# A graph attention and convolution kernel on one core: 136 more columns of el gathered by GpSimd, 34 fewer batches of picks on TensorE

## The chip, the cores and the metric

The kernel runs on one core of a Trainium2 chip. The metric is the device time of one execution in microseconds (us); lower is better. The engines are TensorE (PE, with its weight loads as PEld), VectorE (DVE), ScalarE (ACT), GpSimd (POOL) and SyncE (SP). A "q" behind an engine's name (SPq, POOLq) stands for its sequencer, which issues DMAs.

## The reference

A graph of 6250 nodes with 512 features and 100000 edges, sorted by dst, goes through one attention layer and two convolution layers. What matters for this change is the attention score of every edge:

```python
el = jnp.einsum('nhf,hf->nh', feat_src, attn_l)      # 6250 x 8, one row per node
er = jnp.einsum('nhf,hf->nh', feat_dst, attn_r)
e = el[src] + er[dst]                                # 100000 x 8, one row per edge
e = jnp.where(e >= 0, e, NEG_SLOPE * e)
e_max = jax.ops.segment_max(e, dst, num_segments=N)
exp_e = jnp.exp(e - e_max[dst])
denom = jax.ops.segment_sum(exp_e, dst, num_segments=N)
a = exp_e / jnp.maximum(denom[dst], 1e-16)
msg = feat_v[src] * a[:, :, None]
rst = jax.ops.segment_sum(msg, dst, num_segments=N)
```

After it come layer norm, relu and two layers of `segment_sum((x @ W)[src] * norm, dst)`. The change touches only how `el[src]` is fetched.

## The kernel before, in words

The 100000 edges (padded to 100096) lie as 128 partitions by J = 782 columns; partition p holds edges 782p to 782p + 781. The 6250 nodes are 49 tiles of 128. `el[src]` is an array of 128 x 782 x 8 in the tile `edge`, and it is filled column by column, in two ways:

- **Picks** (columns 0 to PCOLS - 1, PCOLS = J - GCOLS = 764). Four columns (Q) make a batch, so there are 191 batches. SP loads the batch's source numbers, low nine bits, to all partitions (`rows_wmat<-low_tab`, L1107, four buffers). DVE makes three of the four one-hot tiles from them (L683), ACT the fourth (L1371, L1375). PE multiplies them with the table of el, split in three bf16 parts: 4 columns x 4 one-hots x 3 parts = 48 matmuls of 128x128 by 128x104 (L1618), into one of four PSUM banks (the profile's `mm`, `mm`, `tr`, `tr`). DVE then masks the result with the high bits of the source number (L689, semaphore `el_masked`) and reduces it to 8 numbers per edge (L696). DVE and ACT make one-hots up to two batches ahead of PE.
- **Gathers** (columns PCOLS to J - 1, GCOLS = 18). GpSimd issues one indirect DMA per column that fetches 128 rows of 8 numbers from the DRAM table `el_tab` (`collect`, L1236).

The picks stand between a head and a tail. In the head, x is normalised, el and er of each node are made, and the first 14 of 49 "values" (`feat_v` of one tile, L1563) are computed. After the picks, PE goes on with the values, and DVE has the long chain: er spread by scans (L766), scores (L775, L776), a segmented running maximum forwards (L784, then `top_local` for the late columns) and backwards (L798), exp, sums (L809, L822) and the weights. `scores` and the forward scan go over the picked columns first (`early`) and the gathered ones then (`late`), behind `all_landed(dve, el_in, GCOLS)`. Only then do the three large gather-and-add stages start (L1277), one indirect DMA of GpSimd per 128 edges.

What sets the order is the order of each engine's own instructions, written out by hand, with semaphores between engines. Each engine's loop over the batches is a real loop over four batches at a time, with the first batches and the last ones (what does not fill four) written out before and behind it (`pipelined`, L115). GpSimd's queue around the picks is: 18 gathers of el, 49 scatters of er (L1245), four gathers of dst (L1225), one of carry (L1250), `collect(EARLY, GCOLS)`, which is empty, as EARLY = GCOLS, then a wait for the first carry of the DVE chain and a memset (L1255). SP's queue is: 191 loads of low_tab, with the load of er (L1105) ahead of load 104; then three small tables written to DRAM (L1111, L1113) and read back (L1084 to L1089), for which it waits until all gathers of el have landed. The small tables are written in pieces of four bytes.

Of the kernel before, what the change touches and what calls it, by code (L numbers as in the profile page):

```python
# [68 lines left out]
GROUPED = (0, 8, 24, TILES)  # L69
XACT = 3  # L70
AHEAD = 8
GCOLS = 18
PCOLS = J - GCOLS
PB = -(-PCOLS // P)
Q = 4
ZW = 184
KT = 4
NA = -(-TILES // KT)
EARLY = GCOLS
V1 = 14  # L80
V_AT = (V1 + 11, V1 + 19, V1 + 29)
EXP_AT = (V1 + 25, V1 + 25)
# [39 lines left out]
def build(nc, x, src, dst, W_src, b_src, W_dst, b_dst, W_val, b_val, attn_l, attn_r, W1, b1, W2, b2, out):  # L122
    ctx = ExitStack()
    with ctx:
# [192 lines left out]
        def first(t):  # L317
# [39 lines left out]
        low_kept, src_hot_set, el_summed, a_hot_set, el_masked, el_picked = map(sem, (  # L357
            "low_kept", "src_hot_set", "el_summed", "a_hot_set", "el_masked", "el_picked"))
# [38 lines left out]
        def all_landed(eng, pair, count):  # L397
            for b in range(2):
                n = sum(1 for k in range(count) if k // AHEAD % 2 == b)
                if n:  # L400
                    eng.wait_ge(pair[b], 16 * n)
# [26 lines left out]
        def _(dve):  # L428
# [345 lines left out]
            def scores(at):  # L774
                did(dve.tensor_tensor(el[:, at, :], el[:, at, :], top[:, at, :], ALU.add))  # L775
                did(dve.scalar_tensor_tensor(el[:, at, :], el[:, at, :], SLOPE, el[:, at, :], ALU.mult, ALU.max))  # L776
# [9 lines left out]

            all_landed(dve, el_in, GCOLS)
            scores(late)
# [220 lines left out]
        def _(sp):  # L1009
# [71 lines left out]
            def load_tabs():  # L1081
                sp.wait_ge(ends_kept, 16)
                sp.wait_ge(tabs_kept, 48)
                sp.dma_start(ends_row[:, 0:UNITS], ends_tab).then_inc(tabs_in, 16)  # L1084
                for n in range(2):
                    sp.dma_start(slot_row[n], slot_tab[n].rearrange("b p -> (b p)")[0:SP].rearrange(
                        "(a n) -> a n", a=1)).then_inc(tabs_in, 16)
                with nc.allow_non_contiguous_dma(reason="the count of every second step"):
                    sp.dma_start(need_row, need_tab.rearrange("b p -> (b p)")[0:SP].rearrange(  # L1089
                        "(a n two) -> a n two", a=1, two=2)[:, :, 1]).then_inc(tabs_in, 16)  # L1090
# [19 lines left out]
            with nc.allow_non_contiguous_dma(reason="one step of the tables per partition"):  # L1110
                sp.dma_start(need_tab.rearrange("b p -> p b"), need_i[:, :]).then_inc(tabs_kept, 16)  # L1111
                for n in range(2):
                    sp.dma_start(slot_tab[n].rearrange("b p -> p b"), slotcol_i[n][:, :]).then_inc(tabs_kept, 16)  # L1113
            all_landed(sp, el_in, GCOLS)
            load_tabs()
# [64 lines left out]
        def _(pool):  # L1180
# [49 lines left out]

            def collect(lo, hi):
                for n in range(lo, hi):
                    if n % AHEAD == 0 and n >= 2 * AHEAD:
                        pool.wait_ge(el_in[n // AHEAD % 2], n // (2 * AHEAD) * (16 * AHEAD))
                    at = PCOLS + n
                    pool.indirect_dma_start(el[:, at, :], None, el_tab, bass.IndirectOffsetOnAxis(  # L1236
                        ap=src_flat[:, at:at + 1], axis=0)).then_inc(el_in[n // AHEAD % 2], 16)
            collect(0, EARLY)

            pool.wait_ge(er_idx_set, 1)  # L1240
            pool.wait_ge(er_zeroed, 16)
            for t in range(TILES):
# [7 lines left out]
            pool.indirect_dma_start(carry[:, :], None, er_node, bass.IndirectOffsetOnAxis(  # L1250
                ap=dst_i[:, 0:1], axis=0)).then_inc(er_first_in, 16)
            collect(EARLY, GCOLS)

            pool.wait_ge(dve_prep, marks["carry_in"][0])
# [484 lines left out]
```

## Time and profile before

| | us |
|---|---|
| median of 3 runs | 4226.9 |
| lowest and highest | 4221.7, 4226.94 |
| the profiled execution, its own time | 4226.32 |
| its span | 4224.4 |
| PE busy | 3556.3 (84%) |
| POOL busy | 2477.7 (59%) |
| DVE busy | 2342.3 (55%) |
| ACT busy | 1840.1 (44%) |

The span runs from the first to the last instruction of the trace. The page also cuts it into 40 slices of 105.6 us; a digit is the busy share of a slice in tenths. Timelines give the start of a row, its length, the engine, the line of the code, the operation with what it writes and reads, how many there are, and in brackets how long the engine idled before it and what ended that. The chain of waits goes back from the last instruction to whatever released each step.

### The profile page before, as it was taken

How to read it: one execution, taken by the hardware profiler on the slowest of the kernel's cores; microseconds unless marked ns; L12 is line 12 of the kernel's file. 1: busy time of each engine (PE TensorE's matmuls, PEld its weight loads, DVE VectorE, ACT ScalarE, POOL GpSimd, SP SyncE). 2: the span in 40 equal slices, each digit the busy share in tenths (PEclk: the TensorE clock that was granted, in tenths of full speed). 3: DMA queues.
4: the chain of work that ended last, by engine and by line, in shares of the span. 5: the costliest groups of instructions: out<-in, count | busy, mean ns of one | idle time of the engine just before them, and what ended most of it. 6: DMA issues, size and time to landing. Idle time of an engine off the chain costs nothing.

```text
span 4224.4 us, 59337 instructions
## 1 busy us (share of the span) xinstructions
PE 3556.3 (84%) x16793; PEld 1765.3 (42%) x16793; DVE 2342.3 (55%) x4085; ACT 1840.1 (44%) x4240; POOL 2477.7 (59%) x2597
## 2 busy tenths in 40 slices
PE   5899998677788888889678888888997778888887
PEld 4599994322223333344233333333443333333333
DVE  6598889577777888888222323333452222333336
ACT  4366551344545555545333334444343333444442
POOL 3620000277777777754677777777204777777775
PEclk9999999899999999999899999999999999999998
DMA  8722323577777777755777777777315777777779
GB/s 293 232 65 59 87 52 112 204 210 210 210 210 211 210 211 211 210 186 189 210 210 210 210 210 210 210 210 211 104 67 187 211 210 210 210 210 211 210 209 346
DMA packets 319071, 808.16 MB, mean 191 GB/s; under 512 B 69250, under 2 KB 98836, under 8 KB 317826
## 3 DMA queue, kind: packets, MB, share of 16 engines
q0 software_dynamic: 195328, 630.16, 51.3%
q1 hardware_dynamic: 93973, 121.41, 8.9%
q10 hardware_dynamic: 29580, 54.49, 3.7%
q8 instruction: 67, 1.10, 0.1%
q14 instruction: 123, 1.00, 0.1%
HBM read 718.41 MB, written 88.24 MB: 191 GB/s over the span
## 4 chain that ended last, share of the span: by engine, by line
PE 36%; POOL 23%; issue 20%; DMA 11%; DVE 6%; SPq 1%; POOLq 1%; DVEq 1%; ACT 1%; ACTq 0%
POOL edge L1277 18%; PE mm L1526 8%; PE mm L1618 5%; PE tr L1618 5%; DMA edge<-h_tab,src_group 5%; POOL rows_wmat L1277 5%; DMA rows_wmat<-v_tab,src_group 4%; PE sm L1690 4%; PE mm L1690 4%; PE sm L1563 3%; PE tr L1690 2%; DVE edge L865 2%; PE tr L1521 1%; PE hist_ps L1690 1%; DVE big L875 1%
## 5 line engine op out<-in xcount | busy, mean ns | idle before, releaser
L1277 POOL DMA_INDIRECT edge<-h_tab,src_group x1564 | 1483.8, 949 | 711.0 <-issue 447.8
L1433 ACT ACTIVATE hots<-iota,drel 128x128 f32<-128x128 f32 x1760 | 538.0, 388 | 1175.9 <-PE tr L1690 599.2
L1277 POOL DMA_INDIRECT rows_wmat<-v_tab,src_group x782 | 739.2, 945 | 288.2 <-issue 218.7
L1690 PE MATMUL mm<-edge,hots 128*128 x880 | 455.2, 666 | 196.4 <-SPq L1097 193.5
L1690 PE MATMUL sm<-edge,hots 128*128 x880 | 445.9, 654 | 159.8 <-SPq L1097 157.6
L890 DVE TENSOR_TENSOR big<-big,mm 128x512 f32 x220 | 151.2, 687 | 680.2 <-PE tr L1690 663.5
L890 DVE TENSOR_TENSOR big<-big,sm 128x512 f32 x220 | 151.2, 687 | 617.1 <-PE misc L1690 602.7
L1690 PE MATMUL tr<-edge,hots 128*128 x880 | 395.6, 592 | 0.0
L1690 PEld LDWEIGHTS mm<-edge,hots 128*128 128x128 f32 x880 | 179.6, 211 | 464.9 <-issue 464.8
L1526 PE MATMUL mm<-rows_wmat 128*128 128x512 f32 x784 | 355.7, 597 | 0.0
L1690 PEld LDWEIGHTS sm<-edge,hots 128*128 128x128 f32 x880 | 176.7, 208 | 421.5 <-issue 421.4
L1670 PE MATMUL mm<-edge,hots 128*128 128x512 f32 x592 | 275.9, 605 | 62.5 <-ACT hots L1419 39.8
L1670 PE MATMUL sm<-edge,hots 128*128 128x512 f32 x584 | 276.7, 604 | 54.8 <-issue 26.9
L865 DVE TENSOR_TENSOR edge<-rows_wmat,tr 128x1024 f32<-128x1024 f32 x224 | 271.9, 1214 | 85.4 <-SPq L1097 85.3
L1419 ACT ACTIVATE hots<-eler_hots,ones 128x256 f32<-128x256 f32 x440 | 223.6, 508 | 204.9 <-PE sm L1670 77.2
L865 DVE TENSOR_TENSOR edge<-rows_wmat,misc 128x1024 f32<-128x1024 f32 x216 | 262.5, 1215 | 81.4 <-SPq L1097 81.3
L1414 ACT ACTIVATE eler_hots<-iota,drel 128x128 f32<-128x128 f32 x880 | 298.2, 386 | 0.0
L1255 POOL MEMSET big<- 128x8781 f32 x1 | 7.4, 7423 | 449.5 <-DVE carry L723 449.5
L1690 PEld LDWEIGHTS tr<-edge,hots 128*128 128x128 f32 x880 | 167.3, 190 | 212.2 <-issue 212.2
L1436 ACT ACTIVATE hots<-hots,ones 128x1024 f32<-128x1024 f32 x220 | 252.6, 1148 | 7.1
L1618 PE MATMUL mm<-big,edge 128*128 128x104 bf16 x4608 | 226.8, 211 | 11.5 <-issue 6.0
L1618 PEld LDWEIGHTS mm<-big,edge 128*128 128x128 bf16 x4608 | 220.5, 98 | 13.3 <-issue 10.5
(255 smaller groups left out, 4814.8 us busy)
## 6 DMA issues: line engine op xcount, KB each, us to landing
h_tab<-rows_wmat SPq DMA_DIRECT2D x98, 256.0 KB, 2.0
edge<-h_tab,src_group POOLq DMA_INDIRECT x1564, 3.7
rows_wmat<-low_tab SPq DMA_DIRECT2D x191, 128.0 KB, 3.0
ht_tab<-rows_wmat SPq DMA_DIRECT2D x49, 256.0 KB, 4.4
big<-ht_tab ACTq DMA_DIRECT2D x49, 256.0 KB, 2.9
v_tab<-rows_wmat ACTq DMA_DIRECT2D x49, 256.0 KB, 2.9
x_tab<-big SPq DMA_DIRECT2D x49, 256.0 KB, 2.2
rows_wmat<-v_tab,src_group POOLq DMA_INDIRECT x782, 3.7
```

The costliest lines, as they stand in the source:

```text
L865: dve.tensor_tensor(msgs[:, k % MSGS, :, :].rearrange("p c (h f) -> p c h f", f=F), got, weights.unsqueeze(3).to_broadcast([P, 2, H, F]), ...
L890: dve.tensor_tensor(big[:, ds(o, D)], big[:, ds(o, D)], agg_ps[bank][:, :], ALU.add).then_inc(a["acc_added"], 1)
L1277: pool.indirect_dma_start(ring[:, 2 * u + c, :], None, tab, bass.IndirectOffsetOnAxis(ap=src_group[:, n:n + 1], axis=0)).then_inc(a["rows_ ...
L1414: act.activation(dist[:, n % 2, c, :], iota[:, :], ACT.Abs, bias=drel[:, n * 2 + c:n * 2 + c + 1], scale=-1.0).then_inc(a["dist_set"], 1)
L1419: act.activation(onehot[:, n % HOTS, :, :], dist[:, n % 2, :, :], ACT.Relu, bias=ones[:, 0:1], scale=-1.0).then_inc(a["onehot_set"], 1)
L1433: act.activation(group_hots[:, q % 2, e, :], iota[:, :], ACT.Abs, bias=drel[:, col:col + 1], scale=-1.0).then_inc(a["dist_set"], 1)
L1436: act.activation(group_hots[:, q % 2, :, :], group_hots[:, q % 2, :, :], ACT.Relu, bias=ones[:, 0:1], scale=-1.0).then_inc(a["onehot_set"], 1)
L1526: last = nc.tensor.matmul(bank, rows[:, slot, k * P:(k + 1) * P], rhs(k), start=(k == 0), stop=(k == KC - 1))
L1563: last = pe.matmul(sm[par][:, :], ht_ring[:, s.j, k * P:(k + 1) * P], wmat[:, k, 0:D], start=(k == 0), stop=(k == KC - 1))
L1618: last = pe.matmul(sum_ps[bank][:, q * NA * H:(q + 1) * NA * H], src_hot[:, par, kt, q * P:(q + 1) * P], el_parts[:, part, kt, :, :], star ...
L1670: last = pe.matmul(gat_ps[w % GAT_SUMS][:, :], onehot[:, w % HOTS, n, :], msgs[:, w % MSGS, n, :], start=(n == 0), stop=(n == 1))
L1690: last = pe.matmul(agg_ps[bank][:, :], group_hots[:, q % 2, w % GROUP * 2 + n, :], edge[:, ds(slot[w % OFFS] + n * D, D)], start=(n == 0), ...
```

## The change

GCOLS goes from 18 to 154, so PCOLS goes from 764 to 628 and the batches from 191 to 157. EARLY stays at 18 gathers ahead of the scatters. The other 136 gathers come behind the gather of carry, and each of them first waits until VectorE has masked a given number of batches: gather n (from 0) waits for n - 18 + 12 masked batches, so gather 18 for 12 and gather 153 for 147.

```diff
-GCOLS = 18
+GCOLS = 154
 PCOLS = J - GCOLS
 PB = -(-PCOLS // P)
...
-EARLY = GCOLS
+EARLY = 18
+PACED = 12
...
             def collect(lo, hi):
                 for n in range(lo, hi):
+                    if n >= EARLY:
+                        pool.wait_ge(el_masked, n - EARLY + PACED)
                     if n % AHEAD == 0 and n >= 2 * AHEAD:
                         pool.wait_ge(el_in[n // AHEAD % 2], n // (2 * AHEAD) * (16 * AHEAD))
                     at = PCOLS + n
```

GpSimd's instructions behind the scatters of er, before (the first row is the last of the 49 scatters; `dst_rows` and `er_node` are gathers of dst and of carry; the memset of `big` waits for the DVE chain behind the picks):

```order
L1245 DMA er_tab<-eler_hots,er_idx 106368x8 [waits er_scattered0]
L1225 DMA big<-dst_rows,gidx 128x256 [waits dve_prep]
L1225 DMA big<-dst_rows,gidx 128x256 x3
L1250 DMA carry<-er_node,edge 128x8 [waits dst_in,er_kept]
L1255 MEMSET big 128x8781 [waits dve_prep]
L1259 DMA edge<-w_tab,gidx 128x2048 [waits w_kept]
```

And after, the first rows and the last of them:

```order
L1253 DMA carry<-er_node,edge 128x8 [waits dst_in,er_kept]
L1239 DMA edge<-el_tab,src_flat 128x8 [waits el_masked] x6
L1239 DMA edge<-el_tab,src_flat 128x8 [waits el_in1,el_masked]
L1239 DMA edge<-el_tab,src_flat 128x8 [waits el_masked] x7
L1239 DMA edge<-el_tab,src_flat 128x8 [waits el_in0,el_masked]
L1239 DMA edge<-el_tab,src_flat 128x8 [waits el_masked] x7
...
L1258 MEMSET big 128x8781 [waits dve_prep]
L1262 DMA edge<-w_tab,gidx 128x2048 [waits w_kept]
```

All 136 gathers stand between the gather of carry and the memset; every eighth also waits for the landing of an earlier group of eight.

TensorE's end of the picks, before: the loop's last batch and branch, then the batches written out behind the loop, the turning of tables and the values.

```order
L1618 MATMUL tr<-big,edge 128x104 x48
L115 REGISTER_ALU
L115 COMPARE_AND_BRANCH
L1618 MATMUL mm<-big,edge 128x104 x96
L1618 MATMUL tr<-big,edge 128x104 x48
L1629 MATMUL tr<-ident,big 128x128 x8
L1563 MATMUL sm<-rows_wmat,big 128x512 x20
```

And after:

```order
L1621 MATMUL tr<-big,edge 128x104 x48
L116 REGISTER_ALU
L116 COMPARE_AND_BRANCH
L1621 MATMUL mm<-big,edge 128x104 x48
L1632 MATMUL tr<-ident,big 128x128 x8
L1566 MATMUL sm<-rows_wmat,big 128x512 x20
```

Behind the loop stands one batch where there were three; the loop itself turns 38 times where it turned 46 times.

SP's end of the loads, before (load 104 on, with er ahead of it, then the small tables):

```order
L1105 DMA big<-er_tab 128x6256 [waits er_scattered0,er_scattered1,far_dist,src_hot_set]
L1107 DMA rows_wmat<-low_tab 128x512
L1107 DMA rows_wmat<-low_tab 128x512 [waits far_dist,src_hot_set] x86
L1111 DMA need_tab<-need_i 128x4x1
L1113 DMA slot_tab_gat<-slotcol_i_gat 128x4x1
L1113 DMA slot_tab_gcn<-slotcol_i_gcn 128x4x1
L1084 DMA ends_row<-ends_tab 1x391 [waits ends_kept,tabs_kept,el_in1,el_in0]
```

And after:

```order
L1106 DMA big<-er_tab 128x6256 [waits er_scattered0,er_scattered1,far_dist,src_hot_set]
L1108 DMA rows_wmat<-low_tab 128x512
L1108 DMA rows_wmat<-low_tab 128x512 [waits far_dist,src_hot_set] x52
L1112 DMA need_tab<-need_i 128x4x1
L1114 DMA slot_tab_gat<-slotcol_i_gat 128x4x1
L1114 DMA slot_tab_gcn<-slotcol_i_gcn 128x4x1
L1085 DMA ends_row<-ends_tab 1x391 [waits ends_kept,tabs_kept,el_in1,el_in0]
```

The load of er stands at the same batch, 104; behind it 52 loads follow where 86 did.

## Rows read from the trace of the kernel before

**Rows 1.** The page: busy tenths in 40 slices of the span.

```profile
PE   5899998677788888889678888888997778888887
DVE  6598889577777888888222323333452222333336
POOL 3620000277777777754677777777204777777775
```

**Rows 2.** Timeline of PE: picks, two batches to a row, first, 51st pair.

```profile
202.25 6.06 PE L1618 MATMUL mm<-big,edge 128*128 128x104 bf16 x96 [2.90 <-ACT edge L1375]
208.15 4.59 PE L1618 MATMUL tr<-big,edge 128*128 128x104 bf16 x96
...
429.48 4.59 PE L1618 MATMUL tr<-big,edge 128*128 128x104 bf16 x96
```

**Rows 3.** Timeline of POOL: last scatter, last gather before the memset.

```profile
234.86 0.96 POOL L1245 DMA_INDIRECT er_tab<-eler_hots,er_idx x1 [0.30 <-issue]
...
241.19 0.94 POOL L1250 DMA_INDIRECT carry<-er_node,edge x1 [0.30 <-issue]
691.62 7.42 POOL L1255 MEMSET big<- 128x8781 f32 x1 [449.49 <-DVE carry L723]
```

**Rows 4.** Windows: length, then PE, PEld, DVE, ACT, POOL busy, PEclk, DMA share, GB/s.

```profile
210.00:236.00 26.00, 26.00 (x569) 26.00 (x566) 24.37 (x72) 15.73 (x24) 19.73 (x21) 1.00 0.26 64
250.00:276.00 26.00, 26.00 (x568) 26.00 (x566) 23.30 (x72) 15.89 (x24) 0.00 (x0) 1.00 0.27 60
```

**Rows 5.** Timeline of DVE: one-hots beside scatters, then a whole batch without.

```profile
219.41 1.13 DVE L683 TENSOR_SCALAR edge<-rows_wmat,low_id 128x512 bf16<-128x512 f16 x3
...
242.42 0.58 DVE L689 TENSOR_TENSOR rows_wmat<-mm,rows_wmat 128x416 f32<-128x416 f32 x1
...
611.09 0.88 DVE L683 TENSOR_SCALAR edge<-rows_wmat,low_id 128x512 bf16<-128x512 f16 x3 [0.23 <-PE mm L1618]
611.89 0.58 DVE L689 TENSOR_TENSOR rows_wmat<-mm,rows_wmat 128x416 f32<-128x416 f32 x1
612.39 0.57 DVE L696 TENSOR_REDUCE edge<-rows_wmat 128x416 f32 x1
612.88 0.20 DVE L675 TENSOR_TENSOR rows_wmat<-edge,iota 128x52 f32<-128x52 f32 x1
613.30 0.88 DVE L683 TENSOR_SCALAR edge<-rows_wmat,low_id 128x512 bf16<-128x512 f16 x3 [0.22 <-PE tr L1618]
```

**Rows 6.** The load of er at batch 104: SP issues, DVE and PE wait.

```profile
423.95 0.35 SPq L1105 DMA_DIRECT2D big<-er_tab  x1
434.94 0.88 DVE L683 TENSOR_SCALAR edge<-rows_wmat,low_id 128x512 bf16<-128x512 f16 x3 [3.28 <-DMA rows_wmat<-low_tab]
436.65 6.20 PE L1618 MATMUL mm<-big,edge 128*128 128x104 bf16 x96 [2.58 <-ACT edge L1375]
```

**Rows 7.** Timelines of SP and PE at the end of the picks.

```profile
620.04 0.51 SPq L1113 DMA_DIRECT2D slot_tab_gcn<-slotcol_i_gcn  x1
635.41 0.24 SPq L1084 DMA_DIRECT2D ends_row<-ends_tab  x1
...
624.17 0.93 PE L1618 MATMUL mm<-big,edge 128*128 128x104 bf16 x15
...
633.60 4.68 PE L1618 MATMUL mm<-big,edge 128*128 128x104 bf16 x52 [3.19 <-issue]
638.08 2.78 PE L1618 MATMUL tr<-big,edge 128*128 128x104 bf16 x48
643.25 1.19 PE L1629 MATMUL tr<-ident,big 128*128 128x128 f32 x8 [2.39 <-DVE big L739]
```

**Rows 8.** Timeline of DVE behind the picks: scores and scans, early and late.

```profile
659.43 6.52 DVE L775 TENSOR_TENSOR edge<-edge 128x6112 f32<-128x6112 f32 x1
...
673.62 13.23 DVE L784 TENSOR_TENSOR_SCAN edge<-big,edge 128x764 f32<-128x764 f32 x8
686.89 0.31 DVE L775 TENSOR_TENSOR edge<-edge 128x144 f32<-128x144 f32 x1
687.23 0.31 DVE L776 SCALAR_TENSOR_TENSOR edge<-edge 128x144 f32<-128x144 f32 x1
687.58 1.38 DVE L791 TENSOR_TENSOR_SCAN edge<-big,edge 128x18 f32<-128x18 f32 x8
```

**Rows 9.** Line L1236, the gathers of el: time to landing.

```profile
DMA to landing us min/median/max: 3.1/6.1/7.3
```

## The prediction

> **What bounds the kernel now.** The page's slices come first [rows 1]. PE is at 9 tenths or more from the third slice to the sixth, and these are the picks; GpSimd stands at zero there, while its slices behind the eighth are at 7, for it issues the large gathers there. So the stage that the change shortens is one in which PE is full and GpSimd is free, and no later stage lies beside it: the chain of waits passes through the picks on PE, batch after batch, then through VectorE's scans and scores, and only then into the gathers of L1277. Whatever the picks end earlier, everything behind them starts earlier, as long as nothing else is late. The second view is PE's timeline [rows 2]: between the pair of batches that starts at 208.15 and the one at 429.48 there are 50 pairs, 221.33 us, so 4.427 us a pair and 2.213 us a batch of 48 matmuls. In the windows PE is busy 26.00 of 26 us at a granted clock of 1.00, the upper of its two levels [rows 4]. VectorE is near its own limit: a batch of it goes from 611.09 to the end of L675 at 613.08, 1.99 us, with 0.22 us idle before the next [rows 5].
>
> **What the change removes.** 34 batches of picks. On PE they are 34 x 2.213 = 75.3 us, all on the path. VectorE's, ScalarE's and SP's share of these batches lies beside PE's and is worth nothing more.
>
> **What the picks' end adds to that.** The three batches behind the loop do not run at 2.213 us. PE starts the first of them at 624.17, hobbles through 48 matmuls with gaps that are put down to issue, has four of them left at 633.60, and ends the third at 640.86 [rows 7]: 16.7 us where 6.6 would do, a loss of 10.1. SP has just written the three small tables, in pieces of four bytes; its last write is issued at 620.04 and its wait for their landing ends at 635.41. I read the gaps as engines that leave their loops and want new code while DRAM is busy with these pieces. After the change SP's writes stand as far ahead of the last batch as before (it runs four buffers ahead), but only one batch stands behind the loop, so PE leaves the loop two batches, 4.4 us, later with respect to the writes. Two bounds: if the hobbling belongs to the exit, the single batch takes what the first one took, 634.0 - 624.2 = 9.8 us, a loss of 7.6 where it was 10.1, and the saving is 75.3 + 2.5 = 77.8. If it belongs to the writes, PE is released at the same distance from them, some 13.6 us behind 620.04, four matmuls before its end, so at about 634.0 in the old counting where the end was at 640.86: 75.3 + 6.9 = 82.2. The trace shows one case only, so neither is excluded; I take a value nearer to the first, 79, since PE's own gaps begin at the exit and not at the writes.
>
> **What the change adds on GpSimd.** 136 gathers. An indirect DMA of this kind holds GpSimd 0.94 us and the next follows 0.30 us later, 1.25 us each [rows 3], so one per batch of 2.213 us fits. GpSimd has nothing to do between 242.1 and 691.62, 449.49 us of idle time [rows 3], so this lies wholly in a hole. In order: carry is issued at 241.19; the mask at 242.42 is the 17th (the first is at about 207, one per 2.213 us), so gathers 18 to 22 or 23 go at once and the rest one per batch. The last one waits for 147 masks of 157: it is issued some ten batches, 22 us, before the picks end. These gathers have landed in 3.1 to 7.3 us [rows 9]. What waits for them: SP's reading back of the small tables, which is far from late, and VectorE's late scores, which come behind the early scans, 46 us behind the picks' end [rows 7, 8]. What is queued behind them on GpSimd is the memset at 691.62, which waits for VectorE anyway. Cost on the path: 0. If that cover were gone, each gather would cost 1.25 us at most.
>
> **What the gathers do to the picks beside them.** No gather of el runs beside picks in this trace, but 49 scatters of er and five gathers do at the start of the picks, at 1.27 us from one to the next, so 1.7 of them per batch. There PE is full all the same [rows 4]. VectorE is busy 24.37 us of 26 beside 21 of them and 23.30 without: 1.07 / 21 = 0.05 us each. With one per batch that is 0.05 us of the 0.22 us that VectorE has free, so 0 on the path. The other bound is the worst single case: three one-hots took 1.13 us where 0.88 is usual [rows 5], 0.25 us. The mask releases each gather, so all of them meet VectorE at the same point of its batch, and that could make the worst case the rule: 0.25 - 0.22 = 0.03 us by 136 is 4 us. I take 0 to 1 us, because the average of many positions is at 0.05. PE's and ACT's instructions are not longer in that window, and the DMA share is 0.26 beside 0.27, so the loads of low_tab are not slowed either.
>
> **The load of er** (3.1 MB) is issued at 423.95 at batch 104, before and after. The load of low_tab behind it comes late, VectorE waits 3.28 us and PE 2.58 us, and PE's next pair takes 6.20 us and not 4.43 at first [rows 6]: some 4.5 us. Five small gathers now fall beside it. They add little to 3.1 MB; between 0 and 2 us, I take 0.5.
>
> **Head and tail.** VectorE's conversions go over 628 columns and not 764, one transposition and one small DMA fall away in the head; PE works there on the values without waiting for them, so 0. Behind the picks the early part shrinks and the late part grows. Scores: 6112 numbers take 6.52 us and 144 take 0.31, 1.04 ns a number, so the sum stays. Scans: eight of 764 columns take 13.23 us and eight of 18 take 1.38 [rows 8], 1.99 ns a column, so the sum stays too. 0.
>
> **The sum**, against the profiled execution (4226.32 us, span 4224.4, 1.9 us around it; the median of the runs is 4226.9): 4226.3 - 79 + 1 = 4148.3. I forecast 4148.
>
> **A rule that speaks against the change.** The rows show VectorE's one-hots 0.05 us longer for each DMA of GpSimd beside them [rows 4, 5]. The Trainium skill, "SBUF — State Buffer", section "SBUF: two separate sides", says that VectorE and GpSimd share a pair of ports as an exclusive lock: who starts first keeps it for its whole instruction and the other "fully blocks", which in VectorE's two-port modes also starves the descriptors of GpSimd's DMAs. By that rule the sum could come out at the second rival's. The trace does not bear it out at full strength.
>
> **The rivals.**
> 1. *VectorE becomes the pace of the picks.* The gathers are phase-locked to the mask and each costs more than the 0.22 us that are free, say 0.25 to 0.40. Then 135 batches take 0.03 to 0.18 us more, 4 to 24 us: 4152 to 4172. For it: VectorE at 90% and the row of 1.13 us. Against it: 1.7 DMAs a batch did not slow PE. Chance 12%.
> 2. *Slower: GpSimd shuts VectorE out.* Each gather keeps VectorE's one-hots waiting for its whole 0.94 us. VectorE's batch is then 2.93 us, 0.72 us over PE's, by 136: 98 us against 78 saved, so 4246. It is slower than before from 0.58 us a batch over the free 0.22, that is from 0.80 us a gather on. For it: one engine at 90%, and a wait that puts the gather right before the one-hots. Against it: the windows, where the whole of 21 DMAs cost 1.07 us. Chance 3%.
> 3. *The change does not move the end.* The gathers come too late, because every eighth waits for a landing that the load of er holds back, and VectorE waits for the last of them. GpSimd would have to lose over 22 + 46 us for that. Or the picks end earlier and something else is late; I find nothing, as er has landed by 435 and the first picked tables are older. 2%.
> 4. *The end of the picks is cleaner still*: VectorE and ScalarE also leave their loops two batches later, and nobody stalls. Then 75.3 + 10.1 = 85: 4141. 10%.
>
> **How the numbers follow.** The forecast with its bounds (77.8 to 82.2 us saved, less 0 to 4 for contention and the load of er: 4144 to 4153) has 73%. To hold eight in ten I reach to 4140 for the fourth rival, and into the first as far as 4164. Below 4140 I see 4%, above 4164 some 9%. A difference of 0.2%, 8.5 us, is about what a measurement can tell from no change. Faster by more than that: the forecast, rivals 1 and 4, 95%. Within: half of the third and what of the first goes far beyond its bounds, 2%. Slower: 3%.
>
> **What would show it.** In the trace after: 157 batches at 2.21 us a batch in PE's timeline between 250 and 420, at a clock of 1.00; VectorE idle 0.15 to 0.2 us a batch; GpSimd's gathers 2.2 us apart, each released by VectorE's mask, the last at about 535; the picks' end at 559 to 563 and the memset of `big` at 612 to 614 where it was at 691.62; every stage behind it of unchanged length. Wrong would be: pairs of batches over 4.5 us with PE waiting for the one-hots of L683 (rival 1, or 2 if over 5 us); a wait at the load of er well over 3.3 us; a batch behind the loop that takes over 10 us.

## The result, and the profile after

The changed kernel takes 4150.4 us in the median of its four runs beside 4225.7 for the kernel before (a fourth run of it lowers the 4226.9 of the table above); the ratio is 0.9822, with a 95% interval of 0.9808 to 0.9836, so 75 us or 1.8% less. One of the four runs took 5913 us at a granted clock of 0.557; without it the median is 4148.8 (4143.5 to 4152.0), and such runs are left out of the numbers of e4 and e5 below. Forecast were 4148, a range of 4140 to 4164, and faster by over 0.2% with a chance of 95%. The profiled execution took 4152.04 us with a span of 4150.1. Run again on another chip (e0 below) the same kernel took 4148.5 us, at a ratio of 0.9821.

The page's slices answer to [rows 1]. PE's full stretch is shorter, and GpSimd, which stood at 2, 0 and 0 in the third to the fifth slice, is at 5, 4 and 4:

```profile
PE   5899988677888888898788888888997788888887
...
DVE  6599887677777888885222333333552222333336
...
POOL 3654411677777777654777777777106777777775
```

PE's timeline of the picks, in pieces, answers to [rows 2, 6, 7]: the first pair, two rows around the load of er, and the end. (A row is cut where the view's window ends: the pair at 442.37 is 45 matmuls long here.)

```profile
207.55 6.18 PE L1621 MATMUL mm<-big,edge 128*128 128x104 bf16 x96 [2.90 <-ACT edge L1378]
...
434.91 4.59 PE L1621 MATMUL tr<-big,edge 128*128 128x104 bf16 x96
442.37 2.87 PE L1621 MATMUL mm<-big,edge 128*128 128x104 bf16 x45 [2.87 <-ACT edge L1378]
...
550.21 4.59 PE L1621 MATMUL mm<-big,edge 128*128 128x104 bf16 x96
554.64 0.71 PE L1621 MATMUL tr<-big,edge 128*128 128x104 bf16 x12
555.64 0.78 PE L1621 MATMUL tr<-big,edge 128*128 128x104 bf16 x8 [0.29 <-issue]
556.84 0.22 PE L1621 MATMUL tr<-big,edge 128*128 128x104 bf16 x1 [0.42 <-issue]
557.82 2.46 PE L1621 MATMUL tr<-big,edge 128*128 128x104 bf16 x50 [0.76 <-issue]
564.26 2.32 PE L1621 MATMUL tr<-big,edge 128*128 128x104 bf16 x25 [3.97 <-issue]
566.38 4.11 PE L1621 MATMUL mm<-big,edge 128*128 128x104 bf16 x48
```

The picks run from 207.55 to 570.49, 362.9 us, where they ran from 202.25 to 640.86, 438.6 us. That is 75.7 us less, and 34 x 2.213 is 75.3: the batches are gone at their full price, and nearly nothing else happened. Over their ideal (157 x 2.213 = 347.5, before 191 x 2.213 = 422.7) the picks lose 15.4 us, before 15.9. The end of the picks was forecast to be cleaner; it is not. PE starts its last three batches at 554.64 and ends them at 570.49, 15.9 us where 6.6 would do; it was 16.7. From SP's last write of a small table to the end of the picks it is 20.0 us, and it was 20.8.

GpSimd's timeline answers to [rows 3]: carry, the first late gathers, the last ones and the memset.

```profile
246.31 0.94 POOL L1253 DMA_INDIRECT carry<-er_node,edge  x1 [0.30 <-issue]
247.55 0.94 POOL L1239 DMA_INDIRECT edge<-el_tab,src_flat  x1 [0.30 <-issue]
...
538.94 0.94 POOL L1239 DMA_INDIRECT edge<-el_tab,src_flat  x1 [1.40 <-DVE rows_wmat L690]
541.02 0.94 POOL L1239 DMA_INDIRECT edge<-el_tab,src_flat  x1 [1.14 <-DVE rows_wmat L690]
621.17 7.43 POOL L1258 MEMSET big<- 128x8781 f32 x1 [79.20 <-DVE carry L724]
```

Nearly every late gather waits 1.1 to 1.4 us for VectorE's mask, as the pacing wants, and the last one is issued 29 us ahead of the picks' end; 22 were worked out, and the halt at the end of the picks makes up the rest. The memset comes 70.5 us earlier than before. The 5 us that are missing there were lost ahead of the picks, which start at 207.55 and not at 202.25; in e0, which is the same kernel, they start at 201.56, and in the other kernels below between 201.95 and 205.48. So this is the scatter of executions and not the change.

VectorE's windows answer to [rows 4]; the columns are PE, PEld, DVE, ACT and POOL busy, granted clock, DMA share and GB/s:

```profile
302.00:416.00 114.00, 114.00 (x2476) 114.00 (x2474) 107.38 (x311) 68.89 (x104) 48.98 (x52) 1.00 0.28 61
```

PE is full at a granted clock of 1.00 throughout this window. VectorE is busy 94% of the time.

### The profile page after: what moved, and what is told of

Its sections match the earlier page's. It is cut to its first block, busy times and chain, and to the rows that moved or that the text cites. A ratio compares the mean times of both kernels' runs of the same rounds, so it can differ in the third digit from the quotient of the medians.

```text
span 4150.1 us, 55488 instructions
## 1 busy us (share of the span) xinstructions
PE 3489.9 (84%) x15160; PEld 1694.2 (41%) x15160; DVE 2288.9 (55%) x3880; ACT 1798.3 (43%) x4172; POOL 2607.4 (63%) x2733
## 3 DMA queue, kind: packets, MB, share of 16 engines
q14 instruction: 123, 1.01, 0.1%
## 4 chain that ended last, share of the span: by engine, by line
PE 34%; POOL 23%; issue 21%; DMA 12%; DVE 6%; SPq 1%; POOLq 1%; DVEq 1%; ACT 1%; ACTq 0%
POOL edge L1280 17%; PE mm L1529 8%; POOL rows_wmat L1280 5%; DMA edge<-h_tab,src_group 5%; DMA rows_wmat<-v_tab,src_group 4%; PE mm L1621 4%; PE sm L1693 4%; PE tr L1621 4%; PE mm L1693 4%; PE sm L1566 3%; PE tr L1693 2%; DVE edge L866 2%; PE tr L1524 1%; DMA ht_tab<-rows_wmat 1%; PE hist_ps L1693 1%
## 5 line engine op out<-in xcount | busy, mean ns | idle before, releaser
L1693 PE MATMUL mm<-edge,hots 128*128 x880 | 465.9, 679 | 195.3 <-SPq L1098 189.7
L1239 POOL DMA_INDIRECT edge<-el_tab,src_flat x154 | 147.5, 958 | 180.0 <-DVE rows_wmat L690 157.6
L1693 PE MATMUL hist_ps<-edge,hots 128*128 x440 | 206.8, 592 | 0.0
L1693 PE MATMUL misc<-edge,hots 128*128 x440 | 206.8, 592 | 0.0
```

The costliest lines, as they stand in the source:

```text
L1693: last = pe.matmul(agg_ps[bank][:, :], group_hots[:, q % 2, w % GROUP * 2 + n, :], edge[:, ds(slot[w % OFFS] + n * D, D)], start=(n == 0), ...
```

## The experiments

The question after the result was not whether the 34 batches are worth 75 us, but what of the other terms was luck: do the gathers really cost nothing, is the pacing of use, what makes the loss at the picks' end, and how far can it be taken? The theory: the gathers lie in GpSimd's hole and beside PE's picks for free. The rival: they cost a little and something else gives it back.

**e0: the change again**, on the chip of the next three.

> The changed kernel again, beside the others on the same chip: 4150 us, 75 under the kernel before. The gaps of PE, VectorE and ScalarE at the end of the picks begin about 5 us behind the last write of the small tables and cost 10 us, as in both traces so far.

Measured: 4148.5 us (4145.9 to 4150.3), ratio 0.9821 (0.9805 to 0.9838). The end of its picks, and SP's queue beside it:

```profile
548.54 0.50 PE L1621 MATMUL tr<-big,edge 128*128 128x104 bf16 x6
549.41 1.11 PE L1621 MATMUL tr<-big,edge 128*128 128x104 bf16 x20 [0.36 <-issue]
550.92 2.67 PE L1621 MATMUL tr<-big,edge 128*128 128x104 bf16 x49 [0.41 <-issue]
558.94 1.98 PE L1621 MATMUL tr<-big,edge 128*128 128x104 bf16 x21 [5.35 <-issue]
560.71 3.75 PE L1621 MATMUL mm<-big,edge 128*128 128x104 bf16 x48
```

```profile
544.41 0.51 SPq L1114 DMA_DIRECT2D slot_tab_gcn<-slotcol_i_gcn  x1
559.44 0.24 SPq L1085 DMA_DIRECT2D ends_row<-ends_tab  x1
```

PE halts in the two batches that are still in its loop (x6 to x21, 96 matmuls), 5 us behind the last write, and goes on at 558.94, half a microsecond before SP's wait ends. So the exit of the loop is not what it halts at: the exit comes behind the halt. The DMA engines are not busy while it lasts; the last columns here are the granted clock, the DMA share and GB/s:

```profile
547.50:558.50 11.00, 5.31 (x102) 4.77 (x99) 3.01 (x9) 1.76 (x3) 0.00 (x0) 0.92 0.00 0
```

So the packets of the writes are through by 547.3, and what SP waits for until 559.44 is not the moving of the 6 KB.

**e1: no late gathers.** 157 batches of picks, no gathers beside them.

```diff
-            collect(EARLY, GCOLS)
+            pool.memset(edge[:, (PCOLS + EARLY) * H:J * H], 0.0).then_inc(late_zeroed, 1)
```

> The 136 late gathers of el are left out and their columns are set to zero by one memset of GpSimd, so the scores of those edges are not the reference's; picks are 157 batches as in the change. My theory (the gathers lie in GpSimd's hole and cost the picks nothing): 4150, within 3 us of the change, with VectorE's busy time in 302 to 416 falling from 107.4 to about 102.6 us. The rival (the gathers slow the picks or the load of er): faster than the change by 5 us or more.

Measured: 4148.1 us (4146.5 to 4148.7), ratio 0.9818 (0.9802 to 0.9834), 0.4 us from e0. VectorE in the window:

```profile
302.00:416.00 114.00, 114.00 (x2477) 114.00 (x2474) 102.42 (x310) 68.33 (x104) 0.00 (x0) 1.00 0.23 59
```

So 136 gathers cost the path nothing that can be measured. They do cost VectorE something, 102.42 us busy without them and 107.38 with 52 of them, 0.095 each (0.12 in e0, 108.69), and this lies in its idle time.

**e2: no pacing.**

```diff
-                    if n >= EARLY:
-                        pool.wait_ge(el_masked, n - EARLY + PACED)
```

> The wait for el_masked is taken out, so the 136 gathers follow one another at 1.25 us, 1.8 to a batch, from about 247 to 417. My theory (the pacing is not needed, as VectorE has 0.22 us a batch free and a gather takes 0.05 to 0.09 of it): 4150, within 3 us of the change. The rival (VectorE becomes the pace once there are two gathers a batch): pairs of batches over 4.43 us between 250 and 417 and 4 to 20 us more than the change.

Measured: 4145.5 us (4144.6 to 4147.6), ratio 0.9813 (0.9797 to 0.983). GpSimd issues its last gather at 415.56 and not at 535 to 541:

```profile
302.00:416.00 114.00, 114.00 (x2477) 114.00 (x2474) 103.68 (x310) 68.98 (x104) 86.57 (x91) 1.00 0.33 63
```

There are 91 gathers in this window and not 52, and VectorE is busy less, 103.68 us: 0.014 us for each gather. That depends on how the gathers happen to fall on VectorE's batch: in the other kernels whose gathers run freely it is 0.025 (e5), 0.032 (e4), 0.037 (e6) and 0.053 (e9, 107.25 us in all, as much as in the change), and in the paced ones 0.094 (e3) to 0.12 (e0). The pacing is not needed. The difference of 3 us to e0 lies within the intervals, and the traces put it elsewhere: PE is full in this window in both, but in e2 the pair behind the load of er took 4.60 us at a granted clock of 1.00, where it took 6.20 at 0.72 in e0, and the halt at the end cost 7.5 us and not 9.3. So it isn't shown that the pacing costs time either.

**e6: two gathers to a mask.**

```diff
-                        pool.wait_ge(el_masked, n - EARLY + PACED)
+                        pool.wait_ge(el_masked, (n - EARLY) // 2 + PACED + 8)
```

> 154 gathers as in the change, but two of them released by every mask (from mask 20 to 87), so both lie at the same point of VectorE's batch. In the change each gather takes 0.09 to 0.12 us of VectorE's 0.22 free, unpaced ones 0.014. If it is the fixed phase that costs: VectorE's busy time rises to near 26 of 26 us between 260 and 390, pairs of batches stay at 4.43 us or go up to 4.5 (0 to 3 us on the time, 4148 to 4152). If it is the number of gathers that costs: as unpaced, 4146, with VectorE at about 23.6 of 26.

Measured: 4148.4 us (4145.2 to 4149.7), ratio 0.9817 (0.98 to 0.9833), VectorE 105.77 us in 302 to 416 beside 91 gathers, 0.037 each. The design was at fault: two gathers take 2.5 us and a batch 2.2, so GpSimd fell behind the masks and hardly waited for them. In effect it is a second unpaced kernel and says nothing on a fixed phase.

**e10: another phase.** One gather per batch, released by PE's end of the batch.

```diff
-                        pool.wait_ge(el_masked, n - EARLY + PACED)
+                        pool.wait_ge(el_summed, n - EARLY + PACED)
```

> The change with each late gather released by TensorE's end of the batch (el_summed) and not by VectorE's mask, so that it meets VectorE's one-hots from their start. If the phase sets what a gather takes from VectorE: its busy time in 302 to 416 leaves 107 to 108.7 us, up to 110 or more if the whole of the one-hots is met, down to 104 if the end of the gather was what met them; pairs of batches at 4.43 us as long as it stays under 114, and the time 4146 to 4152. If only the number of gathers matters: 107 to 108.7, as in the change.

Measured: 4148.3 us (4146.5 to 4149.8), ratio 0.9824 (0.9807 to 0.984), and in the window

```profile
302.00:416.00 114.00, 114.00 (x2477) 114.00 (x2474) 102.68 (x311) 69.16 (x104) 49.73 (x52) 1.00 0.29 61
```

VectorE is busy as without any gathers. It is the same number of gathers as in the change and they cost 0.005 us each and not 0.1, so it is the phase that sets what they take. The timelines show which part of a gather does it. First GpSimd and VectorE in e10, then in e0:

```profile
306.67 0.94 POOL L1239 DMA_INDIRECT edge<-el_tab,src_flat  x1 [1.60 <-PE mm L1621]
...
306.11 0.88 DVE L684 TENSOR_SCALAR edge<-rows_wmat,low_id 128x512 bf16<-128x512 f16 x3 [0.22 <-PE mm L1621]
```

```profile
307.33 0.94 POOL L1239 DMA_INDIRECT edge<-el_tab,src_flat  x1 [1.73 <-DVE rows_wmat L690]
...
307.38 1.01 DVE L684 TENSOR_SCALAR edge<-rows_wmat,low_id 128x512 bf16<-128x512 f16 x3
```

In e10 a gather starts while the one-hots run and outlives them; they take their 0.88 us. In e0 the one-hots start 0.05 us behind the gather, outlast it by 0.12, and take 1.01. The other batches of this window agree. In e10 the three one-hots nearly always start 0.16 to 0.27 us ahead of a gather and take 0.88 us in every batch. In e0 and in the change they nearly always start behind it: they take 1.02 to 1.10 us when they start 0.2 to 0.3 us behind, 0.88 at about 0.44, 1.08 to 1.12 from 0.47 to 0.5, and 0.95 to 0.98 from 0.6 on. That is what comes out if a one-hot (one every 0.3 us) that would start between some 0.45 and 0.7 us into a gather is held until 0.7. It is read from the rows; no run moved the gathers by known steps.

**e3: the small tables written later.**

```diff
+            sp.wait_ge(el_picked, PCOLS // Q)
             with nc.allow_non_contiguous_dma(reason="one step of the tables per partition"):
```

> SP writes the three small tables only after the last pick is reduced. If the loss of 10 us at the end of the picks belongs to these writes: the 157 batches run to their end at 2.21 us with no gap over 1 us, the picks end 9 to 10 us earlier, and the time is 4140 to 4145, less than the full 10 us since part of the halt then falls on VectorE's scans. If it belongs to the engines leaving their loops: the gaps stay where they are and the time is 4150.

Measured: 4140.3 us (4139.3 to 4143.4), ratio 0.98 (0.9783 to 0.9816), 8.2 us less than e0. The picks run to their end without a gap, and one stands later:

```profile
549.83 4.59 PE L1622 MATMUL tr<-big,edge 128*128 128x104 bf16 x96
554.26 2.38 PE L1622 MATMUL mm<-big,edge 128*128 128x104 bf16 x48
559.03 1.18 PE L1633 MATMUL tr<-ident,big 128*128 128x128 f32 x8 [2.39 <-DVE big L740]
560.04 13.90 PE L1567 MATMUL sm<-rows_wmat,big 128*128 128x512 f32 x32
582.03 5.41 PE L1567 MATMUL sm<-rows_wmat,big 128*128 128x512 f32 x8 [8.09 <-ACT rows_wmat L1362]
```

The loss goes with the writes and not with the loops. It falls now on ScalarE and, through it, on PE's values, 8.09 us, while VectorE is in its long scans and scores; of it 1.95 us reach VectorE (its wait for PE ahead of 587.99), and the rest is hidden.

**e7: every small table written twice.**

```diff
+                for copy in range(2):
+                    to = (need_tab, *slot_tab) if copy else spare_tab
+                    for tab, cols in zip(to, (need_i, *slotcol_i)):
+                        sp.dma_start(tab.rearrange("b p -> p b"), cols[:, :]).then_inc(tabs_kept, 16)
```

> The change with every one of the three small tables written twice, first to a spare place, at the same point of SP's queue. If the halt at the end of the picks is the time in which these writes land: the wait of SP grows from 15 us behind the last write to about 28, the picks end some 13 us later and the time is 4158 to 4164. If it belongs to the loops' exits: 4148 to 4150.

Measured: 4152.3 us (4149.5 to 4155.9), ratio 0.9831 (0.9815 to 0.9847), 4 us more than e6 on the same chip, where 10 to 16 (picks that end 13 us later) were forecast for the writes and none for the exits. SP goes on at 566.63, 24.4 us behind the start of its first write, where it was 16 in e0; but PE halts in 549 to 559, hobbles once more at 566 and ends at 567.3, some 3 us later than in e0. Its last three batches lose 13.3 us (547.34 to 567.31, where 6.6 would do), and kernels with one set lose 7.5 to 9.3. So the halt grows by 4 to 6 us where the wait grows by 8.4: it is not the time in which the writes land. The number missed; the direction stands in the traces, while the times just overlap e6's.

**e8: the same tables in larger pieces.** They are kept in DRAM by partition, 384 pieces of 16 bytes where there were 1536 of 4, at the same place of SP's queue; reading them back then takes 12 DMAs and not three.

```diff
-        need_tab = dram("need_tab", [CUT.blocks, P], I32)
+        need_tab = dram("need_tab", [P, CUT.blocks], I32)
...
-                sp.dma_start(need_tab.rearrange("b p -> p b"), need_i[:, :]).then_inc(tabs_kept, 16)
+                sp.dma_start(need_tab, need_i[:, :]).then_inc(tabs_kept, 16)
```

> The change with the three small tables kept in DRAM by partition, so that they are written in 384 pieces of 16 bytes and not in 1536 of 4 bytes, at the same place of SP's queue, and read back column by column. If the halt at the end of the picks comes from the number of small writes: SP's wait falls from 15 us behind the last write to about 5, the gaps shrink from 10 us to 3 or less, and the time is 4140 to 4143, as with the tables written later. If it comes from any write to DRAM at that point, or from the loops' exits: the gaps stay and the time is 4148 to 4150.

Measured: 4137.7 us (4136.3 to 4138.8), ratio 0.9799 (0.9782 to 0.9815), 10.6 us less than e10 on the same chip and 2.3 us under the range given. SP's queue, and PE beside it:

```profile
543.69 0.43 SPq L1116 DMA_DIRECT2D slot_tab_gcn<-slotcol_i_gcn  x1
547.95 0.24 SPq L1085 DMA_DIRECT2D ends_row<-ends_tab  x1
```

```profile
547.90 4.59 PE L1623 MATMUL tr<-big,edge 128*128 128x104 bf16 x96
552.33 2.37 PE L1623 MATMUL mm<-big,edge 128*128 128x104 bf16 x48
```

The wait falls from 15 us to 4.3 and the halt is gone. It is the small pieces and not a write at that place. The halt's share of the 10.6 us is 9.0 in the profiles (e10 loses 9.2 us in its last three batches, e8 0.2); another 1.6 is the pair behind the load of er, which ran at a granted clock of 1.00 here (4.60 us) and 0.72 in e10 (6.19 us). This pair took 4.60 us in e2, e6 and e7 too and 6.18 to 6.20 in every other kernel, so it goes with neither the gathers nor the writes. Here the tables are read back in pieces of four bytes, hundreds of them, from 548.23 on, and neither PE nor VectorE halts.

**e4: 238 columns gathered,** 136 batches of picks, unpaced (GCOLS = 238, and e2's edit).

> 238 columns gathered, 544 picked (136 batches), no pacing. My theory: 21 batches fewer than in the change at 2.213 us save 46.5 us more, with nothing lost to the gathers: 4148.5 - 46.5 - 1 (no phase lock) = 4101, range 4098 to 4106. The 220 late gathers at 1.25 to 1.26 us run from about 247 to 523, some 10 us past the end of the picks, which VectorE's er scans and early scores cover. The rival (GpSimd's end now sets the late scores, or VectorE becomes the pace): 4110 or more, with VectorE waiting for el ahead of the late scores.

Measured: 4107.5 us (4105.2 to 4108.3), ratio 0.972 (0.9701 to 0.974), on e6's chip, where 154 columns gave 4148.4: 40.8 us saved where 46.5 were forecast, and 1.5 us over the range given. The small tables are written at 497.92 here, while the late gathers still run, and the halt is longer:

```profile
499.79 1.78 PE L1619 MATMUL mm<-big,edge 128*128 128x104 bf16 x35
503.73 0.21 PE L1619 MATMUL mm<-big,edge 128*128 128x104 bf16 x1 [2.17 <-issue]
505.05 0.24 PE L1619 MATMUL mm<-big,edge 128*128 128x104 bf16 x1 [1.11 <-issue]
506.00 2.82 PE L1619 MATMUL mm<-big,edge 128*128 128x104 bf16 x28 [0.71 <-issue]
511.51 0.24 PE L1619 MATMUL mm<-big,edge 128*128 128x104 bf16 x1 [2.69 <-issue]
...
517.40 5.13 PE L1619 MATMUL tr<-big,edge 128*128 128x104 bf16 x96
```

The last four batches take 22.7 us, from 499.79 to 522.53, where 8.9 would do: a loss of 13.9 where e6 loses 8.5 and e0 9.3. The difference to e6 is 5.4 of the 5.7 us that are missing. GpSimd's last gather is issued at 521.50, and VectorE does not wait for it: its late scores come at 561.

**e5: 238 columns and the tables written later.**

> As the kernel with 238 gathers and no pacing, and the three small tables written after the last pick. If the two savings are independent: 8 us less than that kernel, 4093. If the halt behind the writes now also holds back GpSimd's last gathers or the loads behind the picks: less than 4 us gained.

Measured: 4097.6 us (4092.2 to 4103.0), ratio 0.9692 (0.9673 to 0.9712): 9.9 us less than e4, where 8 were forecast for savings that add up. Its three runs lie 11 us apart, all below e4's, so the size is loosely known; in the profiles the picks are 13.3 us shorter, 306.2 and not 319.5.

**e9: 238 columns and the tables in larger pieces.**

> 238 gathers, unpaced, with the tables in pieces of 16 bytes. If the number of small writes causes the halt: 4090 to 4094, since the halt beside the last gathers was longest there, 20 us lost in the picks where the change loses 15. If not: 4105 to 4108.

Measured: 4094.7 us (4092.5 to 4098.3), ratio 0.9694 (0.9678 to 0.971). It is the best version here, with e5 beside it (their runs overlap): 129 us under the kernel before, 54 under the change. It misses the range given by 0.7 us. Against e8 on the same chip, 21 batches fewer gave 43.0 us and not 46.5; in the profiles the first of the large gathers comes 45.0 us earlier. The picks are 44.4 us shorter; of the 2.1 that are missing there 1.6 is again the pair behind the load of er, 6.19 us here and 4.60 in e8.

## Why the prediction was right, point by point

- **34 batches at 2.213 us, 75.3 us, all on the path:** right. The picks are 75.7 us shorter, and the kernel 75 to 77.
- **The picks' end, 2.5 to 6.9 us more, 3.7 taken:** wrong. This is the term that was mis-sized. I read the gaps behind 624 as engines that leave their loops and want code, and argued that a later exit would meet less of it. PE is halted inside its loop (e0), with the tables written later it isn't halted (e3), and with larger pieces not at all (e8). SP's writes stand at the same distance from the last batch before and after, so the loss stayed as it was: 10.1 us before, 9.2 in the profile after. The saving of 3.7 us that the sum takes here measured 0.9, within the scatter of 7.5 to 9.3 us that this loss has in the kernels with 157 batches and the writes at this place (e2, e6, e1, e10, e0). The second bound, that the halt belongs to the writes, had the right cause and drew the wrong conclusion, for it still took the exit for what starts the halt.
- **1 us for contention and the load of er:** e1 puts the gathers at 0.4 us with runs that lie 2 to 4 us apart, so at nothing that can be told. PE waited 2.87 us at the load of er, before 2.58 [rows 6], and 2.17 to 2.87 in all kernels with 157 batches. The slower pair behind it, which the prediction counts as part of the load's 4.5 us, comes and goes with the granted clock: 6.2 us at 0.72, 4.60 at 1.00 (e2, e6, e7, e8).
- **0.05 us of VectorE's time per gather, with 0.25 us as the other bound:** it was 0.094 to 0.12 in the paced kernels. The reason why it could be over the average, that the mask releases every gather at the same point, was right and is shown by e10. I took the average of many phases for a case with a fixed phase; 0.05 is what freely running gathers cost at most (e9, 0.053). It stayed under the 0.22 us that were free, so the first rival didn't come, and nor did the second, the lock for a whole instruction. The Trainium skill, "SBUF — State Buffer", section "SBUF: two separate sides", says that GpSimd and a VectorE operation in a two-port mode block one another fully, for the whole instruction of whichever has the shared ports first. No run here shows in which mode the one-hots run. They are held, but for 0.24 us at most of a gather's 0.94 (1.12 where 0.88 is usual), and those that run in its first 0.4 us are not: the trace does not agree with a lock over the whole of a gather, only with a short one in it.
- **The cover:** right. The last late gather is issued 29 us before the picks end, and the early scores and scans follow; even with 238 of them (e4, e9) VectorE did not wait. VectorE's parts behind the picks shrink and grow as worked out: scores of 5024 numbers take 5.39 us and of 1232 take 1.44, together 6.83, as before [rows 8]. In the change's trace the scans take 10.97 and 3.55 us, together 14.52, before 14.61.
- **The time:** 4148 forecast. By the terms that were right it would have been 4226.3 - 75.3 + 0 to 1 = 4151 to 4152, which is what the profiled execution took; the median is 4150.4, and 4148.5 on the second chip, where the kernel before took 4223.6, so 75 us in both. The forecast saved 78. The error of 4 us in one term is smaller than the scatter of a run. So the range held by its main term, and that the middle of it lies within 2 us of the medians is luck: it holds a saving at the picks' end that did not come.

## What to carry to other kernels

Where one engine is full and another is idle for a long stretch, moving whole units of work to the idle one pays nearly the unit's price on the full engine (75.7 of 75.3 us in the picks here, and 44.4 of 46.5 for the next 21 batches), as long as the neighbour that feeds it has some slack (0.22 us of 2.21 here); count that slack first. Pacing a background engine by its neighbour's progress looks careful but fixes the phase, here at a poor point (0.1 us a gather where another phase cost 0.005 and none at all 0.014 to 0.053), though none of it reached the time: measure one other phase and no pacing at all. And look at every loss at the end of a stage for what happens at the same distance in both kernels, here a few kilobytes written in pieces of four bytes; that loss of 10 us was nobody's instruction in the code that changed.

## What the runs showed of the hardware that I had not expected

- 1536 writes to DRAM of 4 bytes each, 6 KB in all, take 15 us from the last issue to the end of the wait, and PE, VectorE and ScalarE stand still for much of it (PE loses 7.5 to 10 us by it, 13.9 in e4), with gaps put down to issue or to no engine of the core (VectorE 3.33 and 4.48 us in the profile after). The DMA engines' busy share is 0.00 in this stretch (e0). GpSimd does not stand still: in e4 its gathers go on at 1.25 us through the halt, with one wait of 1.29 us. As 384 pieces of 16 bytes they take 4.3 us and nobody stands still (e8). Twice as many pieces of 4 bytes made the wait 8.4 us longer but the halt only 4 to 6 us (e7). Why instructions are held up at all, inside a loop too, stays open: no run here separates the fetching of code from the passing of semaphores. The one packet of the kind "instruction" at the end of e0's picks runs at 561.1, two microseconds behind PE's restart at 558.94, so at least this one is not what PE waited for.
- PE, once halted, goes on at a lower clock: in the profile after, the granted clock is 0.50 from 564.2 to 566.4, the lower of its two levels, and the last 48 matmuls of the picks took 4.11 us at 0.55, where they took 2.38 at 1.00 without a halt (e3). So some 2 us of the halt's price are the clock. In e1 69 matmuls stand between the last gap and these 48, and they took 2.38 as well.
- GpSimd's gathers take 0.94 us beside the picks but 1.43 us beside VectorE's scans of two inputs, in the kernels in which the last gathers reached these (e5, e9):

```profile
520.00 1.44 POOL L1239 DMA_INDIRECT edge<-el_tab,src_flat  x1 [0.31 <-issue]
521.74 1.43 POOL L1239 DMA_INDIRECT edge<-el_tab,src_flat  x1 [0.30 <-issue]
```

  The Trainium skill, "SBUF — State Buffer", section "SBUF: two separate sides", says that a VectorE instruction with two inputs in SBUF contends with GpSimd's reads. The trace agrees that there is contention: a gather takes 0.49 us more. The gathers then follow one another at 1.74 us, and so do the scans (14.01 us for eight, with or without gathers), one gather to a scan. That is what comes out if a gather is held until the running scan ends; that it is held for just this reason was not tested.
